# A sort on VectorE whose exchanges keep half of the keys in PSUM: four operations of 256 columns in place of two of 512

## What is computed

```python
x = x + gnn(_layernorm(x), src, dst, edge_weight, W, b)
#   msgs = features[src] * edge_weight[:, None]
#   agg  = segment_sum(msgs, dst);  agg @ W.T + b
x = x + ffn(_layernorm(x), W_gat, att_src, att_dst, ..., edge_index)
#   e = leaky_relu(a_src[src] + a_dst[dst]); softmax of e over the edges of each dst
#   agg = segment_sum(h[src] * alpha, dst) -> layernorm -> top 2 of 4 experts -> gates
#   out = sum over experts of gate * (gelu(x @ W1 + b1) @ W2 + b2)
```

## Time and profile before

| | us |
|---|---|
| median of three runs | 3680.15 |
| lowest and highest | 3677.34, 3684.65 |
| span of the profiled execution | 3679.4 |
| PE, DVE, ACT, POOL busy in it | 2978.4, 2045.6, 818.5, 2723.6 |

### The profile page before, as it was taken

How to read it: one execution, slowest core, us unless ns; L and a number is a source line. 1 busy time by engine, 2 the same in 40 slices (tenths; PEclk the granted TensorE clock), 3 DMA queues, 4 the chain that set the end, 5 groups by cost and what they waited for, 6 DMA issues and landing times. The chain is left out here.

```text
span 3679.4 us, 60444 instructions
## 1 busy us (share of the span) xinstructions
PE 2978.4 (81%) x13893; PEld 2434.3 (66%) x13894; DVE 2045.6 (56%) x6851; ACT 818.5 (22%) x2320; POOL 2723.6 (74%) x2817
## 2 busy tenths in 40 slices
PE   1475665766857898978999799999999999999548
PEld 1354444554645666656666688888888888888437
DVE  8777678787787666563344223344352434242567
ACT  6300000000101111211222222223222323222247
POOL 6677777777777777777777777777777777777573
PEclk6687887887878999999999899999999999999779
DMA  9643333333433444444444122242222223222289
GB/s 348 196 120 106 107 113 109 112 113 111 118 113 115 120 121 123 126 122 125 127 131 130 52 73 54 56 118 54 73 66 63 57 70 77 55 73 54 54 299 364
DMA packets 276554, 424.71 MB, mean 115 GB/s; under 512 B 59704, under 2 KB 210211, under 8 KB 275363
## 3 DMA queue, kind: packets, MB, share of 16 engines
q0 software_dynamic: 114208, 216.64, 23.5%
q1 hardware_dynamic: 64175, 114.71, 8.5%
q10 hardware_dynamic: 98004, 91.50, 7.6%
HBM read 317.12 MB, written 105.97 MB: 115 GB/s over the span
## 5 line engine op out<-in xcount | busy, mean ns | idle before, releaser
L674 POOL DMA_INDIRECT rows<-feats,src_t x1500 | 1450.4, 967 | 464.4 <-issue 445.9
L1197 POOL DMA_INDIRECT got<-row_dram,src_sorted x1024 | 1000.0, 977 | 312.2 <-issue 312.2
L835 PE MATMUL node_sums<-rows,ys_ahead 128*128 x3904 | 990.9, 408 | 226.0 <-DVE ys_ahead L894 100.6
L835 PEld LDWEIGHTS node_sums<-rows,ys_ahead 128*128 128x128 f32 x3904 | 763.7, 202 | 422.1 <-issue 307.7
L1280 PE MATMUL d_hidden<-d_yt,w 128*128 128x256 f32 x3136 | 713.3, 381 | 7.9 <-DVE d_yt L1365 7.9
L1291 PE MATMUL d_expert<-w,hid 128*128 128x256 f32 x3136 | 708.7, 379 | 0.0
L1280 PEld LDWEIGHTS d_hidden<-d_yt,w 128*128 128x128 f32 x3136 | 595.0, 191 | 88.3 <-DVE d_yt L1365 8.7
L1291 PEld LDWEIGHTS d_expert<-w,hid 128*128 128x128 f32 x3136 | 595.8, 190 | 81.0
L1343 DVE TENSOR_TENSOR yo<-d_expert,x_and_b 128x512 f32<-128x512 f32 x196 | 135.5, 692 | 832.8 <-PE d_expert L1291 825.2
L894 DVE TENSOR_SCALAR ys_ahead<-iota,rel,ew_t 128x128 f32<-128x128 f32 x1952 | 557.5, 364 | 65.3 <-DVE rel L890 2.3
L1225 ACT ACTIVATE hid<-d_hidden,b1c 128x256 f32<-128x256 f32 x784 | 324.3, 471 | 996.5 <-PE d_hidden L1280 793.2
(11 more groups left out here) (299 smaller groups left out, 2271.6 us busy)
## 6 DMA issues: line engine op xcount, KB each, us to landing
y_dram<-yo ACTq DMA_DIRECT2D x196, 256.0 KB, 2.3
ys<-y_dram SPq DMA_DIRECT2D x36, 1024.0 KB, 9.2
rows<-feats,src_t POOLq DMA_INDIRECT x1500
got<-row_dram,src_sorted POOLq DMA_INDIRECT x1024, 2.4
ys_ahead<-y_dram SPq DMA_DIRECT2D x13, 1024.0 KB, 9.0
x_dram<-edge_plan ACTq DMA_DIRECT2D x98, 128.0 KB
d_x<-x_dram ACTq DMA_DIRECT2D x49, 256.0 KB, 3.0
ys_ahead<-in_x ACTq DMA_DIRECT2D x97, 128.0 KB
```

The costliest lines, as they stand in the source:

```text
L674: pool.indirect_dma_start(rows[:, g % RING, j, :], None, feats, bass.IndirectOffsetOnAxis(ap=m.src_t[:, g * GT + j:g * GT + j + 1], axis=0 ...
L835: t = pe.matmul(psA[:, ds(((code >> 1) & 1) * 512, FEAT)], hot[:, r, j, :], rows[:, ds((code >> 2) & (RING - 1), 1), j, :], start=False, s ...
L1197: pool.indirect_dma_start(got[:, k, j, 0:ROWF], None, m.row_dram, bass.IndirectOffsetOnAxis(ap=m.src_sorted[:, BEGIN[b] + j:BEGIN[b] + j + ...
```

## The change

An exchange for a bit above 0 now has four operations of 256 columns. The results whose next bit (the one that the next exchange compares) is 0 go to the SBUF buffer as before; those whose next bit is 1 go to PSUM, to one of the two halves of `psT`, one for even and one for odd bits. The next exchange reads its first input from SBUF and its second from PSUM. The first exchange of each `columns` call reads both from SBUF, and the one for bit 0 writes everything to SBUF with two operations of 512 columns.

```diff
+            def upper(bit):
+
+                n = bit % 2 * (GCOLS // 2)
+                return psT[:, n:n + GCOLS // 2].rearrange("p (a w) -> p a w", w=1 << bit)
+
-            def exchange(buf, bit):
+            def exchange(buf, bit, first):
+
                 to = 1 if buf == 2 else 1 - buf
                 a = key[buf].rearrange("p (a h w) -> p a h w", h=2, w=1 << bit)
                 o = key[to].rearrange("p (a h w) -> p a h w", h=2, w=1 << bit)
-                c.inc(v.tensor_tensor(o[:, :, 0, :], a[:, :, 0, :], a[:, :, 1, :], ALU.min))
-                c.done(v.tensor_tensor(o[:, :, 1, :], a[:, :, 0, :], a[:, :, 1, :], ALU.max))
+                x, y = a[:, :, 0, :], a[:, :, 1, :] if first else upper(bit)
+                if bit == 0:
+                    c.inc(v.tensor_tensor(o[:, :, 0, :], x, y, ALU.min))
+                    c.done(v.tensor_tensor(o[:, :, 1, :], x, y, ALU.max))
+                    return to
+                half = 1 << (bit - 1)
+                u = upper(bit - 1).rearrange("p (a h) w -> p a h w", h=2)
+                for side, op in ((0, ALU.min), (1, ALU.max)):
+                    c.inc(v.tensor_tensor(o[:, :, side, 0:half], x[:, :, 0:half], y[:, :, 0:half], op))
+                    c.inc(v.tensor_tensor(u[:, :, side, :], x[:, :, half:2 * half], y[:, :, half:2 * half], op))
+                v.wait_ge(s_s, c.n)
                 return to
 
             def columns(buf, bits):
                 for bit in range(bits - 1, -1, -1):
-                    buf = exchange(buf, bit)
+                    buf = exchange(buf, bit, first=bit == bits - 1)
                 return buf
```

## The result

| us | before | after |
|---|---|---|
| median of 18 runs each | 3680.07 | 3688.34 |
| lowest and highest | 3676.1, 3684.65 | 3683.72, 3692.59 |
| span of the profiled execution | 3679.4 | 3685.5 |

The ratio is 1.0023, with a 95% interval of 1.0017 to 1.003. The change makes the kernel 8.3 us slower. That is inside the predicted range, but by a little outside the 0.2% (7.4 us) that the prediction counted as no change, which was its likeliest case, at 3680. That case was wrong.

What follows compares the result with a forecast made beforehand. POOL's chain of gathers was taken as the bound: +3.9 us at its wait for PE and -4.1 behind it give -0.2 on the 3679.4 span; with the median 0.75 above the span, 3680 us, range 3669 to 3693.

Steps and rivals of the forecast that it cites:

- likeliest case: Whole kernel: forecast of 3680 us, all within the 0.2% (7.4 us) counted as no change, chance 0.52.
- POOL's chain: First stage: POOL's row gathers run as one chain, 0.95 + 0.30 = 1.25 us each, and set the pace.
- the single gate at group 224 and step 237: Near 1175 us: POOL's gather for group 224 must wait for PE's step 237, one wait of about 9 us.
- the relief under operations that read PSUM: Gathers beside the 129 split exchanges are no longer held up: 0.075 us an exchange, at most 9.7 us.
- Strided SBUF operands cost nothing either (691 to 695 ns at all bits): Sort exchanges on DVE: stepping through SBUF operands was taken to add no time at any bit.
- e = 0.16 us: Extra DVE time of each of the 129 split exchanges, 0.155 to 0.16 us; 20.6 us in all.
- PE's lateness at 610 us: At 609.89 PE waits 2.64 us for rows, so DVE's extra 3.4 us is hidden and PE gains POOL's 1.6.
- The margin: Before the change, POOL's gather at 1178.06 left 3.1 us after the end of step 237, reckoned at 1174.9.
- Rival 2: Operations that touch PSUM cost 0.04 us more each, e = 0.32: 8.5 us slower, 3689; chance 0.22.
- point of decision: The extra per exchange, e = 0.30, from which the kernel is slower by more than 0.2%.
- Rival 1: DVE pays nothing or little for four operations, e = 0: 8.8 us faster, 3671, or 3670 without gate; chance 0.18.
- Rival 3: POOL's gathers are held under the new operations as before, nothing is won: +5.5 us, 3686; chance 0.08.

Runs made afterwards that it cites:

- after_eased_b: The change, with the one-hots for the counts moved so that nine of the 64 come behind the gate, against before: 3674.53 beside 3684.85 us, ratio 0.9972.

## Why the prediction was wrong

**The bound and the place were right.** POOL's chain, the single gate at group 224 and step 237, the relief under operations that read PSUM, and its passing on to the end all stand in the traces. So do the untried costs of PSUM: 433 ns for a write and 421 to 432 with its 8-byte stride, beside 426 in SBUF. The Trainium skill's rule that speaks against the change ("VectorE: DVE Perf Modes", the section on the TRN2 errata: a fixed 120 cycles for an operation from PSUM and 58 for one from SBUF) is not seen here: 256 columns take 420 ns with one input from PSUM and 426 with both from SBUF.

**The step that failed is "Strided SBUF operands cost nothing either (691 to 695 ns at all bits)".** The rows were true, but for the forms of the kernel before, where the SBUF step of a single column never exceeded 8 bytes. Halving the operand at bit 1 makes single columns at 16 bytes. I took e = 0.16 us for all 129 exchanges; measured are 1.45 to 1.46 - 1.33 = 0.13 for the 107 of bits from 2 up (a little under what I took) and 2.17 - 1.33 = 0.84 for the 22 of bit 1. In pieces 7 to 15, 46 exchanges of 0.13 and 8 of 0.84 are 12.7 us, where I had 54 x 0.16 = 8.6. From the start behind piece 7 to the start behind piece 15 (40 and 7 of them, 11.1 us) PE lost 539.4 - 528.7 = 10.8 us. These are PE's two starts behind piece 7, before and then after:

```profile
644.05 8.19 PE L835 MATMUL node_sums<-rows,ys_ahead 128*128 x23 [13.15 <-DVE ys_ahead L894]
```

```profile
646.87 8.45 PE L835 MATMUL node_sums<-rows,ys_ahead 128*128 x25 [14.58 <-DVE ys_ahead L894]
```

**PE's lateness at 610 us had the wrong sign.** I put PE at -1.6, held by rows and therefore moving with POOL. In after the same step starts at 611.34, +1.45: PE came later than its rows there, and the wait of 2.64 us that was to absorb DVE's extra is gone. This hangs on bit 1 too: by the measured prices the 15 + 6 long exchanges of pieces 1 to 6 cost 15 x 0.13 + 6 x 0.84 = 7.0 us, where I had 3.4. That this is all of it is argued, not isolated by a run. 1.45 + 12.2 from there on is the measured 13.6 us; I had -1.6 + 8.6 = 7.0.

```profile
611.34 1.99 PE L835 MATMUL node_sums<-rows,ys_ahead 128*128 x8 [0.25 <-issue]
```

**The margin was 1.1 us, not 3.1.** I divided 8.91 us by four steps for the end of step 237, but the clock is not the same over them. This is the step alone, the first eight records, in before:

```profile
1172.70 3.46 PE L835 MATMUL node_sums<-rows,ys_ahead 128*128 x8 [1.22 <-DVE ys_ahead L894]
```

In windows of L835 (us, PE busy, weight loads busy, granted clock, DMA share, GB/s) PE runs at 0.50, its level of 1.2 GHz, after it has stood still, and at 1.00 later. Before, then after:

```profile
1174.00:1175.00 1.00, 1.00 (x4) 0.73 (x4) 0.50 0.33 90
1175.00:1176.00 1.00, 1.00 (x4) 0.86 (x3) 0.64 0.32 90
1176.00:1177.00 1.00, 1.00 (x6) 0.89 (x5) 1.00 0.31 102
```

```profile
1190.00:1191.00 1.00, 1.00 (x4) 0.82 (x3) 0.50 0.00 0
1191.00:1192.00 1.00, 1.00 (x4) 0.80 (x4) 0.58 0.00 0
1192.00:1193.00 1.00, 1.00 (x6) 0.89 (x5) 1.00 0.42 111
```

In after the step takes 3.78 us, as the low clock lasts longer, and POOL's gather starts 0.79 us after its end. With the same 0.79 before, the gather could have left at 1172.70 + 3.46 + 0.79 = 1176.95; it left at 1178.06. So the gate moved by 13.6 + 0.3 - 1.1 = 12.8 us, as measured. The 0.3 us of clock I had counted as nothing.

**POOL's relief was a little low.** The 832 gathers ahead of the gate are 6.5 us less busy in all and the 668 behind it 5.9 us (windows of L674 with its busy time, before and then after), against 5.7 and 4.1 by 0.075 an exchange; by 75 and 54 exchanges it is 0.09 and 0.11. What came ahead of the gate was lost in the wait, as foreseen.

```profile
100.00:1178.05 1078.05, 803.77 (x832) 0.80 0.41 118
1178.05:2100.00 921.95, 646.62 (x668) 0.93 0.41 118
```

```profile
100.00:1190.85 1090.85, 797.25 (x832) 0.78 0.40 117
1190.85:2100.00 909.15, 640.77 (x668) 0.93 0.41 120
```

**The sum again with the measured terms:** +12.8 at the gate, -5.4 behind it, +7.4 at the last gather, a span longer by 6.1 and a median by 8.3.

**The rivals.** Rival 2 gave 3689, and 3688.34 was measured, but not by its mechanism: nothing that touches PSUM is slower. That its number fits is luck. Its point of decision was e = 0.30 as a mean; the measured mean in pieces 7 to 15 is 12.7 / 54 = 0.24, and the smaller margin and the missing catch-up did the rest. Rival 1 fell with the 1.45 us of an exchange, yet its remark on a kernel with no gate, -9.7 us, is close to what after_eased_b shows (-10.3, from -14 to -6). Rival 3 fell with the gathers of 0.95 us.

## What to carry to other kernels

When an operation is cut into parts, look at the access pattern of each part at every size of the loop, not at the whole's: a price read for runs of two says nothing of single elements, and it was the smallest size, 8 exchanges of the 54 in pieces 7 to 15, that made 6.7 of the 12.7 us that DVE took longer there. Where a ring ties two engines, work out the place with the smallest margin with the clock at that place and the time that the waiting engine needs to start (here 0.79 us), and then see whether some other work can be moved behind it: alone that wins nothing, with the change it turned +8.3 us into -10.3.

## What the hardware showed that I had not expected

An f32 `tensor_tensor` of 256 columns takes 614 to 626 ns as soon as one SBUF operand, input or output, has single elements 16 bytes apart (an input at 32 bytes: 614), and 424 to 426 at 8 bytes; pairs of columns 16 bytes apart cost nothing (bit 1 in before, 512 columns in 691 to 695 ns). PSUM at 8 bytes costs nothing (421 and 432); single elements 16 bytes apart in PSUM were not tried.

Beside dependent groups of two-input operations from SBUF, indirect gathers keep step with the groups, one to each: 1.02 us a gather with an exchange of 1.33, 1.16 with one of 1.46. With one input from PSUM they take 0.95 and keep their own period of 1.25.

PE's granted clock was 0.50 for 5.5 us after its idle stretch of 15 us in after (until about 1191.85), and for 3.0 us after the one of 13 us in before.
